# A graph network kernel on one core: the two gathers of a pair wait for the rows of different earlier pairs

## The chip, the cores and the metric

The kernel runs on one core of one Trainium2 chip, in one launch. The metric is the device time of that core in microseconds (us), from three runs of the kernel: median 1267.71 us, from 1265.4 to 1268.62 us. One more execution was recorded by the hardware profiler, and every row below comes from it.

## What is computed

The input is 1250 nodes of 512 features and 20000 edges, sorted by their target node (`dst`). The target nodes are drawn so that low numbers have far more edges. Two graph layers follow each other; the change touches only the scores of the first, an attention over edges (GATv2):

```python
xl = (x @ Wl).reshape(-1, HEADS, C)            # HEADS = 8, C = 64
xr = (x @ Wr).reshape(-1, HEADS, C)
h = jax.nn.leaky_relu(xl[src] + xr[dst], NEG_SLOPE)
e = jnp.einsum('ehc,hc->eh', h, att)           # the score of each edge and head
m = jax.ops.segment_max(e, dst, num_segments=N_NODES)
ex = jnp.exp(e - m[dst])
denom = jax.ops.segment_sum(ex, dst, num_segments=N_NODES)
msg = (ex / (denom[dst] + 1e-16))[..., None] * xl[src]
out = jax.ops.segment_sum(msg, dst, num_segments=N_NODES)
```

After it come a layer norm, a two-layer perceptron with a gelu, and three graph convolutions, all untouched.

## The kernel before, in words

The work is written out by hand, engine by engine: `gpsimd`, `tensor`, `scalar`, `vector` and `sync` each hold the program of one engine, which it runs in the order in which it is written. Engines meet only through counting semaphores. A `Count` is a semaphore with the number that it will have reached; `wait_ge(x.sem, k)` holds an engine until `x` has been raised k times.

The edges are laid in 22528 slots: blocks of 128 target nodes, each padded to whole *pairs*. A pair is 2 x 128 slots, and there are NG = 88 pairs. The left rows (`xl`, 512 numbers and 8 more for the linear part of the score, 520 in all) lie in a table in HBM, `left_table`. The slots that hold no edge read one and the same row of it.

The score stage does, for each pair n:

- GpSimd (`gather`, L567 to L580): two indirect DMAs, one for each 128 slots, which fetch 128 rows of 520 floats each (266240 bytes) into one of DEPTH = 6 buffers `gathered`. Before the first of them it waits until the buffer is free (`sources_kept`, L577), and, from pair 3 on, until `rows_added` has reached n - LEAD + 1 with LEAD = 3, that is until TensorE has added the rows of pair n - 3 (L579). The second gather of a pair has no wait of its own.
- ScalarE (`seed`, L1003 to L1011): waits for both gathers and copies the 128 x 1024 gathered numbers into two of the six PSUM banks of a ring of three pairs (L1010), and the 16 linear numbers aside (L1011, `sources_kept`). After each even pair it also makes the one-hot matrices for the two pairs to come (`target_hots`, L995 and L1000), for which TensorE must have spread the local target numbers (`spread_local`, L695).
- TensorE (`add_right`, L698 to L716): adds the right rows `xr[dst]` to the two banks, as four matmuls of 128x512 (L705: a high and a low part for each bank), and raises `rows_added`; then two small matmuls for the linear part (L714). Ahead of every second pair it does `spread_local` (four matmuls, L695).
- VectorE (L1493 to L1500): waits for `rows_added` of its pair, then multiplies the positive part by the attention vector (L1497) and sums over the channels (L1499).

The wait on `rows_added` at L579 protects no data: the buffers are guarded by `sources_kept`. It limits how far GpSimd runs ahead.

After the stage a softmax over the edges of each target follows, then the message stage, which fetches all the rows again with the same function `gather` (L581 to L586), there without a wait on `rows_added`. Its first six pairs are fetched at the end of the score stage.

Of the kernel before, what the change touches and what calls it, by code (L numbers as in the profile page):

```python
# [52 lines left out]
def build(nc, ins, out):  # L53
# [23 lines left out]
    GROUPS = [range(0, 3), range(3, 7), range(7, NB)]  # L77
    DEPTH = 6

    LEAD = 3  # L80
    DEN = 2 * HEADS + 2
    SPLITS = 2
    TW = D + HEADS
# [15 lines left out]
    with ExitStack() as ctx:  # L99
# [313 lines left out]
        seeded, rows_added, rows_weighted, pair_scored = count("seeded"), count("rows_added"), count("rows_weighted"), count("pair_scored")  # L413
# [120 lines left out]
        def gpsimd(g):  # L534
            g.memset(eps[:, :], LN_EPS).then_inc(*eps_ready.up())
            g.wait_ge(*eps_ready.now())
            g.memset(x_in[PAD_FROM:P, NB - 1, :], 0.0).then_inc(*padded.up())
            g.wait_ge(*padded.now())
            g.memset(back, 0.0).then_inc(*zeros_ready.up())
            g.iota(digits[:, DIGITS_BY_VECTOR:LOW, :], [[1, LOW - DIGITS_BY_VECTOR], [0, EJ]], base=DIGITS_BY_VECTOR, channel_multiplier=0,  # L540
                   allow_small_or_imprecise_dtypes=True).then_inc(*digits_low.up())
            g.memset(ident[:, :], 0.0).then_inc(*go.up())
            g.memset(ones[:, :], 1.0).then_inc(*go.up())
            g.wait_ge(*go.now())
            g.affine_select(out=ident[:, :], in_=ident[:, :], compare_op=ALU.not_equal, fill=1.0,
                            base=0, pattern=[[-1, P]], channel_multiplier=1)
            g.affine_select(out=earlier, in_=ones[:, :], compare_op=ALU.is_ge, fill=0.0,
                            base=-1, pattern=[[1, P]], channel_multiplier=-1)
            g.iota(iota[:, :], [[1, max(NC, EJ)]], base=0, channel_multiplier=0, allow_small_or_imprecise_dtypes=True)
            g.memset(zero[:, :], 0.0)  # L550
            g.iota(minus_own[:, :], [[0, 1]], base=0, channel_multiplier=-1, allow_small_or_imprecise_dtypes=True)
            g.iota(iota_four, [[1, max(NC, EJ)], [0, QUARTET]], base=0, channel_multiplier=0, allow_small_or_imprecise_dtypes=True)
            g.iota(iota_node, [[1, NP]], base=0, channel_multiplier=0, allow_small_or_imprecise_dtypes=True).then_inc(*constants.up())
            g.iota(digits[:, LOW:HIGH, :], [[1, HIGH - LOW], [0, EJ]], base=LOW, channel_multiplier=0,
                   allow_small_or_imprecise_dtypes=True).then_inc(*digits_high.up())

            def scatter(nth):

                g.wait_ge(d_zeros, 32)
                g.wait_ge(moves_ready.sem, 2 * nth + 2)  # L560
                for j in range(SHARE):
                    g.indirect_dma_start(out=moved[nth], out_offset=bass.IndirectOffsetOnAxis(ap=place_i[R0, j:j + 1], axis=0), in_=moving[R0, j, :],  # L562
                                         in_offset=None).then_inc(d_moved[nth], 16)
            scatter(0)
            scatter(1)

            def gather(n):  # L567
                for i in range(2):
                    c = 2 * n + i
                    g.indirect_dma_start(out=gathered[n % DEPTH][:, i, :], out_offset=None, in_=left_table,  # L570
                                         in_offset=bass.IndirectOffsetOnAxis(ap=src_of[:, c:c + 1], axis=0)).then_inc(d_gather[n % DEPTH], 16)
            g.wait_ge(slots_ready.sem, 1)
            for i in range(2):
                g.wait_ge(d_tile[i], 16 * (NB // 2))
            for n in range(NG):
                if n >= DEPTH:
                    g.wait_ge(sources_kept.sem, n - DEPTH + 1)  # L577
                if n >= LEAD:
                    g.wait_ge(rows_added.sem, n - LEAD + 1)  # L579
                gather(n)  # L580
            for n in range(NG):  # L581
                if n < DEPTH:
                    g.wait_ge(sources_kept.sem, max(k for k in range(NG) if k % DEPTH == n) + 1)
                else:
                    g.wait_ge(message.sem, n - DEPTH + 1)
                gather(n)  # L586


            g.wait_ge(flag_ready.sem, 1)
            g.wait_ge(counts_apart.sem, NB - 1)  # L590
            rounded = [counts_rounded.up() for _ in range(NB)]

            def round_counts():
                for b in range(NB):
                    g.wait_ge(hidden_done.sem, ROUND_FROM + b)
                    g.tensor_copy(counts_r[:, b, :], counts[:, b, :]).then_inc(*rounded[b])  # L596

            def keep_counts():
                for b in range(NB):
                    g.wait_ge(most_turned.sem, 1)  # L600
                    if b:
                        g.wait_ge(counts_rounded.sem, b)
                    g.memset(most[:, :], 0.0).then_inc(*rounded[b])
            g.cond(g.value_load(exact_flag[0:1, 0:1], min_val=0, max_val=1), round_counts, keep_counts)
# [1258 lines left out]
        with nc.Block() as block:  # L1863
            block.vector(vector)
            block.scalar(scalar)
            block.tensor(tensor)
            block.gpsimd(gpsimd)
            block.sync(sync)
# [24 lines left out]
```

## Time and profile before

| what | value |
|---|---|
| median of three runs | 1267.71 us (1265.4 to 1268.62) |
| the profiled execution | 1267.25 us |
| its span, first to last instruction | 1265.2 us, so 2.05 us lie outside it |
| score stage, first to last L1497 | 231.8 to 498.1 us of the span |
| busy in the span: TensorE, VectorE, ScalarE, GpSimd | 87%, 81%, 54%, 36% |
| L570, all 352 gathers of both stages | 375.7 us busy, mean 1067 ns; idle before them 206.2 us |
| L1497, 88 of 128x1024 | 107.8 us busy, mean 1225 ns |
| L1499, 88 | 107.4 us busy, mean 1220 ns |
| L1010, 88 of 128x1024 | 90.4 us busy, mean 1028 ns |

A GpSimd row of a gather lasts while GpSimd issues it; the data land later. A row of the timeline gives the start and the length of an instruction, and in brackets how long its engine sat idle before it and what ended that idle time. "issue" there means that the profile shows no releaser. Where an instruction waits for several semaphores, the profile names the one that it takes to be last, and this can be the wrong one: behind L570 it names L1011, whose semaphore had long been raised.

### The profile page before, as it was taken

The page shows a single profiled execution, that of the slowest core. Times are in us where ns is not written, and L with a number is a line of the kernel's source. Part 1 is how long each engine was busy: PE and PEld are TensorE (multiplying, and loading weights), DVE is VectorE, ACT ScalarE, POOL GpSimd, SP SyncE. Part 2 cuts the span into 40 slices and gives each one's busy share as a digit, 9 for nine tenths or more (in the row PEclk, how much of TensorE's full clock was granted, in tenths as well). Part 3 has the DMA queues.
Part 4 walks back from the last instruction along what each step waited for, and adds up shares of the span by engine and source line. Part 5 has one row for each costly group of instructions (what it writes and reads, how often), then busy time and mean ns, then how long its engine had stood idle before and what let it go on. Part 6 is the DMA issues. An engine that isn't in the chain of part 4 may idle for free.

```text
span 1265.2 us, 15650 instructions
## 1 busy us (share of the span) xinstructions
PE 1103.2 (87%) x4847; PEld 815.4 (64%) x4847; DVE 1028.0 (81%) x1458; ACT 678.8 (54%) x1257; POOL 455.9 (36%) x412
## 2 busy tenths in 40 slices
PE   4979878667777775399999999699999999999998
PEld 2578456555556564255555555488888889889896
DVE  8999999778777887899999999876767769573934
ACT  4601200566565663388888888766564674232320
POOL 2072062666665666267777775000002100000000
PEclk9989989676665665599999999799999999999999
DMA  5000000666666667166676776400000111000002
GB/s 189 34 10 15 26 10 7 168 174 175 176 179 169 174 175 183 37 189 194 194 195 195 196 195 142 142 1 26 1 9 26 65 54 31 1 28 15 1 1 83
DMA packets 43434, 122.82 MB, mean 97 GB/s; under 512 B 7838, under 2 KB 8626, under 8 KB 43352
## 3 DMA queue, kind: packets, MB, share of 16 engines
q0 software_dynamic: 29184, 93.81, 28.0%
q1 hardware_dynamic: 14168, 27.98, 6.6%
q8 instruction: 44, 0.72, 0.2%
q14 instruction: 38, 0.31, 0.1%
HBM read 116.13 MB, written 5.59 MB: 96 GB/s over the span
## 4 chain that ended last, share of the span: by engine, by line
PE 46%; ACT 19%; DVE 14%; DMA 7%; issue 7%; POOL 4%; ACTq 1%; SPq 1%; DVEq 0%; POOLq 0%
PE bank L851 11%; PE bank L811 8%; PE bank L797 8%; ACT counts L1037 7%; PE bank L867 7%; DMA arena<-left_table,arena 7%; PE bank L654 5%; POOL arena L570 4%; ACT hot L924 4%; ACT arena L922 4%; PE bank L705 3%; ACT bank L1010 2%; DVE counts L1252 2%; PE bank L759 2%; PE bank L770 1%
## 5 line engine op out<-in xcount | busy, mean ns | idle before, releaser
L570 POOL DMA_INDIRECT arena<-left_table,arena x352 | 375.7, 1067 | 206.2 <-issue 101.6
L759 PE MATMUL bank<-arena,hot 128*128 128x512 f32 x352 | 177.6, 620 | 4.0 <-DVE den_parts L1587 4.0
L705 PE MATMUL bank<-xr_hi,hot_t 128*128 x176 | 114.1, 649 | 73.1 <-ACT bank L1010 50.1
L1497 DVE SCALAR_TENSOR_TENSOR arena<-bank,arena 128x1024 f32<-128x1024 f32 x88 | 107.8, 1225 | 52.3 <-PE bank L705 32.6
L1010 ACT ACTIVATE bank<-arena 128x1024 f32<-128x1024 f32 x88 | 90.4, 1028 | 95.3 <-DMA arena<-left_table,arena 87.3
L851 PE MATMUL bank<-counts_r,ns 128*128 128x512 f32 (+2 forms) x720 | 137.1, 349 | 0.0
L851 PEld LDWEIGHTS bank<-counts_r,ns 128*128 128x128 f32 x720 | 125.6, 188 | 10.4
L1037 ACT ACTIVATE counts<-bank 128x1280 f32 x88 | 108.9, 1238 | 35.0 <-issue 25.8
L770 PE MATMUL bank<-arena 128*128 128x512 bf16 x528 | 113.1, 351 | 0.5 <-ACT counts L1037 0.3
L1499 DVE TENSOR_REDUCE arena<-arena 128x16 f32<-128x1024 f32 x88 | 107.4, 1220 | 3.0
L705 PEld LDWEIGHTS bank<-xr_hi,hot_t 128*128 128x128 f32 x176 | 50.2, 285 | 92.2 <-issue 84.5
L1583 DVE TENSOR_TENSOR arena<-arena 128x1024 f32<-128x1024 f32 x88 | 107.3, 1219 | 0.0
L562 POOL DMA_INDIRECT moved<-counts x32 | 57.7, 1802 | 129.8 <-DVE counts L1301 61.5
L654 PE MATMUL bank<-arena 125*125 125x160 f16 (+1 forms) x576 | 89.8, 332 | 13.9 <-DVE arena L1320 13.9
L760 PE MATMUL bank<-den_parts,hot 128*128 128x18 f32 x176 | 101.9, 579 | 0.0
L705 PE MATMUL bank<-xr_lo,hot_t 128*128 x176 | 100.5, 571 | 0.0
L654 PEld LDWEIGHTS bank<-arena 125*125 125x125 f16 (+1 forms) x576 | 74.9, 157 | 29.2 <-DVE arena L1320 17.4
L1595 DVE TENSOR_SCALAR arena<-arena 128x1280 bf16<-128x1280 f16 x176 | 89.5, 551 | 0.0
L770 PEld LDWEIGHTS bank<-arena 128*128 128x128 bf16 x528 | 52.6, 117 | 53.5 <-ACT counts L1037 14.0
L596 POOL CAST counts_r<-counts 128x1280 fp32r<-128x1280 f32 x10 | 13.6, 1356 | 202.3 <-issue 170.9
L759 PEld LDWEIGHTS bank<-arena,hot 128*128 128x128 f32 x352 | 53.8, 193 | 34.8 <-issue 26.0
L633 PE MATMUL bank<-arena 128*128 128x512 f32 x160 | 75.4, 624 | 0.8 <-ACT arena L917 0.8
(248 smaller groups left out, 2193.8 us busy)
## 6 DMA issues: line engine op xcount, KB each, us to landing
arena<-left_table,arena POOLq DMA_INDIRECT x352
arena<-in_x_dram SPq DMA_DIRECT2D x18, 256.0 KB, 4.6
arena<-in_L_gnn_W_dram SPq DMA_DIRECT2D x8, 512.0 KB
arena<-in_L_gnn_W_dram SPq DMA_DIRECT2D x2, 1536.0 KB, 10.7
arena<-in_L_gnn_W_dram SPq DMA_DIRECT2D x3, 1024.0 KB, 5.2
left_table<-arena SPq DMA_DIRECT2D x10, 260.0 KB, 2.0
out_dram<-state SPq DMA_DIRECT2D x9, 256.0 KB
arena<-in_L_gnn_Wl_dram SPq DMA_DIRECT2D x1, 1024.0 KB, 9.8
```

Of the source, the lines that this page charges most:

```text
L570: g.indirect_dma_start(out=gathered[n % DEPTH][:, i, :], out_offset=None, in_=left_table, in_offset=bass.IndirectOffsetOnAxis(ap=src_of[:, ...
L654: ins_ = t.matmul(bank[0:out_rows, psum, 0:width], rows[R0, at[0], 0:out_rows, at[1]], pick_col[n % 2][R0, at[0], 0:width, at[1]], start=( ...
L705: ins_ = t.matmul(bank[:, 2 * (n % ZRING) + i, :], mine, part[:, bass.ds(at, 1), :].rearrange("p b n -> p (b n)"), start=False, stop=(part ...
L759: t.matmul(bank[:, psum, :], as_float(hot[c % 4]), w[:, i, :], start=(i == 0), stop=(i == 1))
L760: t.matmul(bank[:, psum + 1, 0:DEN], hot[c % 4], den_parts[:, c, :], start=(i == 0), stop=(i == 1)).then_inc(*tile_summed.up())
L770: ins_ = t.matmul(flat[:, COUNT_AT + at:COUNT_AT + end], low_hot[n // 2 % 2][:, :, c % QUARTET], code_hot[c % 4][:, at:end], start=(c == 0 ...
L851: ins_ = t.matmul(bank[:, SUM_BANKS[part][k], 0:n], lhs, rhs, start=(s == 0 and half == 0), stop=(s == NB - 1 and half == 1))
L1010: a.activation(bank[:, at:at + 2, :], gathered[n % DEPTH][:, :, 0:D], ACT.Copy).then_inc(*seeded.up())
L1037: a.activation(counts[:, :, bass.ds(at * P, P)], flat[:, COUNT_AT:COUNT_AT + NP].rearrange("p (b n) -> p b n", n=P), ACT.Copy).then_inc(*c ...
L1497: v.scalar_tensor_tensor(y, bank[:, at:at + 2, :], 0.0, over(att_relu, 1, 2), ALU.max, ALU.mult).then_inc(*rows_weighted.up())
L1499: v.tensor_reduce(sc, y.rearrange("p i (h c) -> p (i h) c", c=C), AX.X, ALU.add).then_inc(*pair_scored.up())
L1583: v.tensor_tensor(w.rearrange("p i (h c) -> p i h c", c=C), gathered[s][:, :, 0:D].rearrange("p i (h c) -> p i h c", c=C), over(weights[:, ...
```

## The change

The one number LEAD = 3 becomes a pair of numbers, 4 for the first gather of a pair and 3 for the second. The wait moves from ahead of the pair into the loop over its two gathers. In the message stage `gather` is called without them and stays as it was.

```diff
-    LEAD = 3
+    LEADS = 4, 3
...
-            def gather(n):
+            def gather(n, rows=None):
+
                 for i in range(2):
                     c = 2 * n + i
+                    if rows and n + 1 - rows[i] > 0:
+                        g.wait_ge(rows_added.sem, n + 1 - rows[i])
                     g.indirect_dma_start(out=gathered[n % DEPTH][:, i, :], out_offset=None, in_=left_table,
                                          in_offset=bass.IndirectOffsetOnAxis(ap=src_of[:, c:c + 1], axis=0)).then_inc(d_gather[n % DEPTH], 16)
...
             for n in range(NG):
                 if n >= DEPTH:
                     g.wait_ge(sources_kept.sem, n - DEPTH + 1)
-                if n >= LEAD:
-                    g.wait_ge(rows_added.sem, n - LEAD + 1)
-                gather(n)
+                gather(n, LEADS)
```

On GpSimd's queue of before, from the seventh gather on (pair 3), the waits stand at the first gather of each pair; `sources_kept` joins from pair 6 on:

```order
L570 DMA arena<-left_table,arena 128x520 [waits tile1_out,tile0_out,slots_ready]
L570 DMA arena<-left_table,arena 128x520 x5
L570 DMA arena<-left_table,arena 128x520 [waits rows_added]
L570 DMA arena<-left_table,arena 128x520
L570 DMA arena<-left_table,arena 128x520 [waits rows_added]
L570 DMA arena<-left_table,arena 128x520
L570 DMA arena<-left_table,arena 128x520 [waits rows_added]
L570 DMA arena<-left_table,arena 128x520
L570 DMA arena<-left_table,arena 128x520 [waits rows_added,sources_kept]
L570 DMA arena<-left_table,arena 128x520
```

The same place after the change (its lines are numbered three higher):

```order
L573 DMA arena<-left_table,arena 128x520 [waits tile1_out,tile0_out,slots_ready]
L573 DMA arena<-left_table,arena 128x520 x6
L573 DMA arena<-left_table,arena 128x520 [waits rows_added] x5
L573 DMA arena<-left_table,arena 128x520 [waits rows_added,sources_kept]
L573 DMA arena<-left_table,arena 128x520 [waits rows_added]
```

One gather more (the first of pair 3) goes without a wait; after it every gather of the stage has a wait on `rows_added`, and the second one of a pair has that alone. No instruction changes its place, on GpSimd or on another engine.

## Rows read from the trace of the kernel before

The windows give, for each stretch, its length and then for TensorE, its weight loads, VectorE, ScalarE and GpSimd the busy time and the number of instructions, then the granted TensorE clock (1.00 is 2.4 GHz, 0.50 is 1.2 GHz), the share of the DMA engines and the GB/s. The waits give the engine and line that waited, for whom, the sum in us, how often, and the longest.

**Rows 1.** Page, part 4: the chain that ended last, by line.
```profile
PE bank L851 11%; PE bank L811 8%; PE bank L797 8%; ACT counts L1037 7%; PE bank L867 7%; DMA arena<-left_table,arena 7%; PE bank L654 5%; POOL arena L570 4%; ACT hot L924 4%; ACT arena L922 4%; PE bank L705 3%; ACT bank L1010 2%; DVE counts L1252 2%; PE bank L759 2%; PE bank L770 1%
```

**Rows 2.** Waits between 230 and 500 us.
```profile
ACT bank L1010 <- DMA arena<-left_table,arena: 87.3, 61, 3.3
...
PE bank L705 <- ACT bank L1010: 50.1, 52, 2.5
DVE arena L1497 <- PE bank L705: 32.6, 43, 1.8
```

**Rows 3.** Timeline of VectorE, L1497 of pair 3 and of pair 87.
```profile
239.41 1.23 DVE L1497 SCALAR_TENSOR_TENSOR arena<-bank,arena 128x1024 f32<-128x1024 f32 x1
...
498.06 1.23 DVE L1497 SCALAR_TENSOR_TENSOR arena<-bank,arena 128x1024 f32<-128x1024 f32 x1 [1.54 <-PE bank L705]
```

**Rows 4.** Timeline, one round of the loop: L1497 of pair 27 to that of pair 30.
```profile
312.26 1.23 DVE L1497 SCALAR_TENSOR_TENSOR arena<-bank,arena 128x1024 f32<-128x1024 f32 x1 [1.04 <-PE bank L705]
...
312.91 0.95 POOL L570 DMA_INDIRECT arena<-left_table,arena  x1 [1.32 <-ACT counts L1011]
...
314.17 0.94 POOL L570 DMA_INDIRECT arena<-left_table,arena  x1 [0.30 <-issue]
...
317.91 1.03 ACT L1010 ACTIVATE bank<-arena 128x1024 f32<-128x1024 f32 x1 [2.30 <-DMA arena<-left_table,arena]
...
319.18 0.79 PE L705 MATMUL bank<-xr_hi,hot_t 128*128 x1 [0.70 <-issue]
...
321.36 1.23 DVE L1497 SCALAR_TENSOR_TENSOR arena<-bank,arena 128x1024 f32<-128x1024 f32 x1 [0.98 <-PE bank L705]
```

**Rows 5.** Windows: the whole stage from pair 3 on, and four stretches.
```profile
239.40:498.10 258.70, 189.37 (x669) 149.69 (x666) 205.41 (x169) 155.40 (x255) 161.19 (x171) 0.61 0.66 176
302.00:308.90 6.90, 3.75 (x21) 2.94 (x20) 6.10 (x6) 4.43 (x8) 4.90 (x6) 0.99 0.70 184
308.90:325.90 17.00, 13.08 (x44) 10.56 (x45) 13.05 (x11) 10.43 (x18) 9.79 (x11) 0.50 0.65 175
...
490.50:503.00 12.50, 4.82 (x15) 3.78 (x13) 9.59 (x9) 2.71 (x5) 9.75 (x10) 0.50 0.83 219
...
473.00:494.00 21.00, 15.90 (x49) 12.43 (x47) 15.61 (x13) 10.31 (x18) 13.33 (x15) 0.50 0.77 161
```

**Rows 6.** Timeline, the step from L1010 to L1497 at the full clock (pair 26).
```profile
306.17 1.03 ACT L1010 ACTIVATE bank<-arena 128x1024 f32<-128x1024 f32 x1 [1.82 <-DMA arena<-left_table,arena]
...
308.74 1.23 DVE L1497 SCALAR_TENSOR_TENSOR arena<-bank,arena 128x1024 f32<-128x1024 f32 x1 [0.48 <-DVE arena L1499]
```

**Rows 7.** Timeline: L1497 of pair 0, and the gather that waits for its rows.
```profile
231.79 1.22 DVE L1497 SCALAR_TENSOR_TENSOR arena<-bank,arena 128x1024 f32<-128x1024 f32 x1 [1.71 <-PE bank L705]
...
232.02 0.95 POOL L570 DMA_INDIRECT arena<-left_table,arena  x1 [3.83 <-PE bank L705]
```

**Rows 8.** Timeline: two L1497 with VectorE never idle between them.
```profile
258.45 1.23 DVE L1497 SCALAR_TENSOR_TENSOR arena<-bank,arena 128x1024 f32<-128x1024 f32 x1 [0.61 <-PE bank L705]
...
260.96 1.23 DVE L1497 SCALAR_TENSOR_TENSOR arena<-bank,arena 128x1024 f32<-128x1024 f32 x1
```

**Rows 9.** Timeline: from the rows of pair 27 over the one-hots to pair 29.
```profile
312.24 0.61 PE L695 MATMUL bank<-arena 128*128 128x128 bf16 x4
...
312.89 0.69 ACT L995 ACTIVATE arena<-bank,minus_own 128x512 f32<-128x512 f32 x1 [0.34 <-PE bank L695]
...
313.69 0.72 ACT L1000 ACTIVATE hot_t<-arena,ones 128x512 fp32r<-128x512 f32 x1
...
314.44 1.03 ACT L1010 ACTIVATE bank<-arena 128x1024 f32<-128x1024 f32 x1
...
317.90 1.23 DVE L1497 SCALAR_TENSOR_TENSOR arena<-bank,arena 128x1024 f32<-128x1024 f32 x1 [0.59 <-PE bank L705]
```

**Rows 10.** Timeline of GpSimd: first and last of nine gathers issued without a wait.
```profile
490.51 0.94 POOL L570 DMA_INDIRECT arena<-left_table,arena  x1 [0.31 <-issue]
...
500.53 0.95 POOL L570 DMA_INDIRECT arena<-left_table,arena  x1 [0.30 <-issue]
```

## The prediction

> **What bounds the kernel now.** I began with the chain that ended last [rows 1]. Of its parts 7% (the data of the gathers on their way), 4% (L570, issuing gathers), 3% (L705) and 2% (L1010) have to do with the stage that the change touches. No compute engine fills this part of the chain: the stage goes at the pace of a round trip. The waits of the stage say the same and show the direction [rows 2]: ScalarE's copy L1010 waits 87.3 us in 61 waits for gathered data, TensorE's L705 waits 50.1 us for that copy, VectorE's L1497 waits 32.6 us for L705. What is late first is the gather.
>
> How long is a pair? L1497 runs once for each pair. From pair 3 to pair 87 are 84 pairs, from 239.41 to 498.06 us [rows 3]: 258.65 us, so 3.08 us for each. From here on "pace" is this number.
>
> Why 3.08? One round trip can be read off the timeline [rows 4]. L1497 of pair 27 begins at 312.26, just as the rows of its pair are done. GpSimd was waiting for these rows and starts the first gather of pair 30 at 312.91 (+0.65), the second at 314.17 (+1.26), ScalarE copies at 317.91 (+3.74, the second gather from its issue to its use; ScalarE sat idle 2.30 us for it), L705 begins at 319.18 and L1497 of pair 30 at 321.36 (+3.45 from the copy). Together 9.10 us for three pairs, since the wait goes three pairs back: 3.03 for one. The measured 3.08 is this loop and 0.05 us for each pair of irregularity. The loop bounds the stage, and the first gather's issue is part of it, although only the second one's data come last.
>
> **The change part by part.** No instruction is added on any engine but the waits, and the gathers, their size and their order stay. What changes is when GpSimd may begin each gather. Name T(n) the start of L1497 of pair n.
>
> 1. The second gather of pair n may begin at T(n-3) plus a wake-up; the first one has gone before it, since it needs only T(n-4). So the 1.26 us of the first issue leave the loop. The first gather itself: T(n-4) + 0.65 + 1.26 is earlier than T(n-3) + 0.2 at any pace above 1.7, so it does not hold up the second.
>
> 2. The wake-up. With two semaphores to wait for it takes 0.65 [rows 4]. The second gather will wait for one alone. The nearest row is the gather of pair 3, which waits for `rows_added` alone: L1497 of pair 0 begins at 231.79, the gather at 232.02 [rows 7], so 0.23. The bounds are 0.23 and 0.65; I take 0.23. The new loop is 0.23 + 3.74 + 3.45 = 7.42 for three pairs, 2.47 for one (2.61 with the dear wake-up). The saving by the loop alone would be 9.10 - 7.42 = 1.68 in three pairs, 0.56 in one. Less than that will arrive, because three other limits lie just below 3.08, and the largest of them takes over:
>
> 3. VectorE. When it is never idle, two L1497 are 258.45 to 260.96 apart [rows 8]: 2.51. GpSimd. Nine gathers issued without a wait, 490.51 to 500.53 [rows 10], are 10.02 / 8 = 1.25 apart, 2.50 for a pair. The extra wait adds nothing when it is already fulfilled, as far as the rows show (the 1.26 in rows 4 is an issue after a two-semaphore wait). In the queue, behind a second gather that waits stands the first one of the next pair: it begins at T(n-3) + 0.23 + 1.25, and the second one after it at T(n-3) + 2.73, against its own release at T(n-2) + 0.23. At a pace of 2.51 both fall together, so GpSimd just keeps up and cannot make up for a delay.
>
> 4. ScalarE and TensorE together. After each even pair ScalarE makes one-hots from a product of TensorE that stands behind the rows of the pair before. With TensorE at the low clock [rows 9]: the rows of pair 27 are there (T = 312.26), L695 runs at 312.24, L995 waits for it and starts at 312.89, L1000 at 313.69, only then the copy of pair 29 at 314.44, and T(29) is 317.90. That is 5.64 us for two pairs, a pace of 2.82, and no earlier gather shortens it. With the full clock the last step is 2.57 (306.17 to 308.74 [rows 6]) in place of 3.45, which alone takes the 5.64 to 4.76, a pace of 2.38 and below VectorE's.
>
> So the pace after the change hangs on TensorE's clock: 2.82 at 1.2 GHz, 2.51 at 2.4 GHz. Before, the granted clock is 0.61 over the stage [rows 5], that is the high level for 22% of the time. In a stretch at the high level TensorE was busy 3.75 of 6.90 us (54%) and it then fell; in one at the low level 13.08 of 17.00 us (77%), and it stayed low [rows 5]. How does the density change? At the low level, 77% at 3.08 becomes 84% at 2.82; at the high one, 54% becomes 66% at 2.51. Both go towards the high level. I take the high level for 0.4 of the time: 0.4 x 2.51 + 0.6 x 2.82 = 2.70. The irregularity of 0.05 should shrink, because a late transfer now finds slack: 3 x 2.82 - 7.42 = 1.04 us at the low level, and at the high one, where the loop is 0.88 shorter, 3 x 2.51 - 6.54 = 0.99. I leave 0.01 of it and take 2.71. Saving: 84 x (3.08 - 2.71) = 31 us. The start gives some more: the first gather of pair 3 no longer waits until 232.02, one issue of 1.25 us in the path to T(3). Sum 32.
>
> The Trainium skill, in "TensorE: Matmul & The Clock Gate" (Part 1: The HAM clock gate), says that the throttled state is the default, that a busy stretch releases it and an idle one brings it back. The direction is that of the two windows above; by that rule alone, with a TensorE that is idle a third of the time at a pace of 2.51, either level could hold, and the saving would be 18 us at the low one and 44 us at the high one, as in the first two rivals.
>
> 5. What comes behind the stage. The six pairs fetched ahead for the message stage are issued after it and are not waited for until the softmax is through; they start earlier by what the stage gains. The softmax and the message stage keep their lengths. So what the stage gains, the end gains.
>
> The sum is made against the profiled execution: 1267.25 us (span 1265.2 and 2.05 outside), less 32 is 1235.2. The median of the runs is 0.46 above that execution; so the prediction is 1235.7.
>
> **The rivals.**
>
> A. The clock stays mostly low. For it: 0.50 for 17 us at a stretch at 77% [rows 5]. Against it: the higher density. Pace 2.82 and 0.05, saving 84 x 0.21 = 18 us: 1250.
>
> B. The clock stays mostly high: 2.51 and 0.05, saving 84 x 0.52 = 44 us: 1224. For it: at the high level every limit other than VectorE and GpSimd is well below 2.51. Against it: it fell at 54%, and 66% isn't far from that.
>
> C. The transfers don't keep up. A pair is 2 x 266240 bytes, at 2.51 us 212 GB/s, where the stage has had 176 [rows 5]. Against it: while gathers were issued at 1.25, 219 GB/s were moved, with the DMA engines 83% busy [rows 5]. If some 190 GB/s is all that holds over a long stretch, the pace is 2.80 and 0.05: saving 19 us, 1248.
>
> D. No change. The copy waits for both gathers, and if the second one's landing depended on something other than its issue, an earlier issue would only lie longer in the queue. The +3.74 would become 3.74 + 1.68, and the time 1268. Against it: DMA engines at 66% busy [rows 5] are idle between the gathers.
>
> E. Slower. More gathers are under way at once, and they hinder each other. In the last pairs of the stage, whose slots read one and the same row, the DMA engines were 77% busy and moved only 161 GB/s [rows 5]. If more transfers in flight pulled the whole stage to that, a pair would take 532480 / 161 = 3.31 us, 84 x 0.23 = 19 us more: 1287. It decides from the point where the rate falls under 532480 / 3.08 = 173 GB/s. Against it: the 219 GB/s, with as many in flight as GpSimd can issue.
>
> **How the numbers follow.** The forecast (a mixed clock) has a chance of 0.47, A 0.16, B 0.18, C 0.10, D 0.05, E 0.04. Faster by over 0.3% (3.8 us, about what the runs can tell from none) are the first four: 0.91. Within 0.3%: 0.05. Slower: 0.04. The likeliest case gives 1235.7. The range goes from B with a little more (1222) to A and C (1252).
>
> **What would show it.** In the profile after: L1497 from pair 3 to 87 in 228 us or so, not 258.65; the second gathers starting 0.2 to 0.3 after an L1497, the first ones 1.25 after the second gather before; L1010's wait for gathered data well under 87.3 us, and in its place ScalarE waiting for L695 and VectorE idle less; the granted clock of the stage above 0.61, at 0.7 to 0.75; 195 to 205 GB/s. I am wrong in step 1 if the time from the second gather to the copy grows by more than a few tenths; in step 2 if the second gathers start 0.65 after L1497 (this alone would cost little); in step 4 if the pace is under 2.8 in stretches at the low clock.

## The result, and the profile after

| | before | after |
|---|---|---|
| median of the runs, us | 1268.16 (4 runs, 1265.4 to 1270.19) | 1234.64 (4 runs, 1232.33 to 1235.81) |
| ratio, 95% interval | | 0.9735 (0.971 to 0.9759) |
| profiled execution, its span | 1267.25, 1265.2 | 1235.52, 1233.6 |
| first gather of the stage to the start of the last sum over the channels | 279.5 us | 247.8 us |
| the softmax behind it | 30.2 us | 30.3 us |
| the message stage, its gathers | 248.1 us | 247.7 us |
| from the last gather to the end | 487.6 us | 487.5 us |

The whole gain of the profiled executions (31.6 us of span) lies in the score stage (31.7 us), as step 5 had it. Ratios leave out slow runs, of which there was one (leads_3_3 below: 1770.64 us at a granted clock of 0.552). In the new kernel the lines are one further down from L571 on: the copy is L1011, the rows L706, VectorE's product L1498; a gather is L573.

VectorE's timeline, product of pair 0, 3 and 87 (start, length, engine, line, and in brackets the idle time before it and what ended it), kernel after:

```profile
231.45 1.22 DVE L1498 SCALAR_TENSOR_TENSOR arena<-bank,arena 128x1024 f32<-128x1024 f32 x1 [0.82 <-PE bank L706]
...
239.95 1.22 DVE L1498 SCALAR_TENSOR_TENSOR arena<-bank,arena 128x1024 f32<-128x1024 f32 x1
...
466.91 1.23 DVE L1498 SCALAR_TENSOR_TENSOR arena<-bank,arena 128x1024 f32<-128x1024 f32 x1 [0.99 <-PE bank L706]
```

From pair 3 to 87 that is 226.96 us and a pace of 2.70, against 258.65 and 3.08 in [rows 3]. Of the 84 distances between two products 64 are 2.51 to 2.55, those of a VectorE that is hardly ever idle; before there were 17.

The waits of the kernel after between 230 and 470 us (sum, times, longest), which answer to [rows 2]:

```profile
PE bank L706 <- ACT bank L1011: 68.4, 58, 3.1
...
ACT bank L1011 <- DMA arena<-left_table,arena: 45.2, 46, 2.5
...
ACT arena L996 <- PE bank L696: 19.3, 22, 1.9
DVE arena L1498 <- PE bank L706: 18.2, 21, 1.6
```

The copy's wait for data is down from 87.3 to 45.2 us, VectorE's from 32.6 to 18.2, and ScalarE waits 19.3 us for the product that it makes the one-hots from.

One delay and what follows it, timeline of the kernel after:

```profile
247.65 0.95 POOL L573 DMA_INDIRECT arena<-left_table,arena  x1 [0.30 <-issue]
...
252.53 1.22 DVE L1498 SCALAR_TENSOR_TENSOR arena<-bank,arena 128x1024 f32<-128x1024 f32 x1
...
253.20 1.03 ACT L1011 ACTIVATE bank<-arena 128x1024 f32<-128x1024 f32 x1 [1.63 <-DMA arena<-left_table,arena]
...
256.65 1.22 DVE L1498 SCALAR_TENSOR_TENSOR arena<-bank,arena 128x1024 f32<-128x1024 f32 x1 [1.64 <-PE bank L706]
256.81 0.94 POOL L573 DMA_INDIRECT arena<-left_table,arena  x1 [1.80 <-PE bank L706]
...
257.27 0.69 ACT L996 ACTIVATE arena<-bank,minus_own 128x512 f32<-128x512 f32 x1 [1.61 <-PE bank L696]
```

The second gather of pair 9 is issued at 247.65 and its copy begins 5.55 us later, where [rows 4] have 3.74: a transfer that is late, and VectorE stands still for 1.64 us. GpSimd, which in most rounds issues without a stop, waits for the rows of pair 9 and goes on 0.16 us after the product has begun. This is the second gather of pair 12, released three pairs back, with the cheap wake-up of [rows 7].

Windows of the kernel after: the stage from pair 3 to about 82, the rest with its last five pairs, then two stretches at the low clock and one at the high one (columns as in [rows 5]):

```profile
239.90:447.50 207.60, 149.41 (x627) 120.99 (x626) 191.79 (x158) 147.29 (x240) 148.34 (x157) 0.75 0.73 201
447.50:466.90 19.40, 12.43 (x40) 9.83 (x38) 13.53 (x12) 8.00 (x14) 12.85 (x14) 0.59 0.99 195
...
280.30:290.60 10.30, 9.15 (x30) 7.39 (x31) 8.84 (x8) 6.00 (x10) 6.87 (x8) 0.50 0.68 188
417.24:425.30 8.06, 6.98 (x23) 5.76 (x24) 7.33 (x6) 5.05 (x10) 5.67 (x6) 0.50 0.76 217
328.10:334.90 6.80, 3.92 (x22) 3.14 (x22) 6.63 (x6) 5.43 (x9) 5.28 (x6) 1.00 0.73 201
```

In the long window VectorE is busy for 92% (191.79 of 207.60), and the clock is at 0.75, where the stage had 0.61. The last five pairs are another matter: DMA engines busy 99%, VectorE 70%.

### The profile page after: what moved, and what is told of

It reads as the page before. It is cut to its first block, busy times and chain, and to the rows that moved or that the text cites. A ratio compares the mean times of both kernels' runs of the same rounds, so it can differ in the third digit from the quotient of the medians.

```text
span 1233.6 us, 15630 instructions
## 1 busy us (share of the span) xinstructions
PE 1073.8 (87%) x4827; PEld 796.7 (65%) x4847; DVE 1027.9 (83%) x1458; ACT 679.6 (55%) x1257; POOL 455.7 (37%) x412
## 4 chain that ended last, share of the span: by engine, by line
PE 49%; ACT 22%; DVE 15%; DMA 6%; issue 4%; POOL 2%; ACTq 2%; SPq 1%; DVEq 0%; POOLq 0%
PE bank L852 11%; PE bank L812 9%; PE bank L798 8%; ACT counts L1038 8%; PE bank L868 7%; PE bank L655 5%; DMA arena<-left_table,arena 5%; PE bank L706 4%; ACT hot L925 4%; ACT arena L923 4%; ACT bank L1011 3%; POOL arena L573 2%; DVE counts L1253 2%; PE bank L760 2%; ACT hot_t L1001 1%
## 5 line engine op out<-in xcount | busy, mean ns | idle before, releaser
L573 POOL DMA_INDIRECT arena<-left_table,arena x352 | 376.2, 1069 | 173.6 <-issue 93.9
L706 PE MATMUL bank<-xr_hi,hot_t 128*128 x176 | 102.7, 584 | 68.8 <-ACT bank L1011 68.4
L1498 DVE SCALAR_TENSOR_TENSOR arena<-bank,arena 128x1024 f32<-128x1024 f32 x88 | 107.7, 1224 | 20.7 <-PE bank L706 18.2
L1011 ACT ACTIVATE bank<-arena 128x1024 f32<-128x1024 f32 x88 | 90.4, 1028 | 49.3 <-DMA arena<-left_table,arena 45.2
L771 PE MATMUL bank<-arena 128*128 128x512 bf16 (+1 forms) x508 | 109.6, 348 | 2.4 <-DVE arena L1596 0.4
L706 PEld LDWEIGHTS bank<-xr_hi,hot_t 128*128 128x128 f32 x176 | 45.4, 258 | 83.1 <-issue 76.3
L706 PE MATMUL bank<-xr_lo,hot_t 128*128 x176 | 89.5, 509 | 0.0
```

Of the source, the lines that this page charges most:

```text
L706: ins_ = t.matmul(bank[:, 2 * (n % ZRING) + i, :], mine, part[:, bass.ds(at, 1), :].rearrange("p b n -> p (b n)"), start=False, stop=(part ...
L771: ins_ = t.matmul(flat[:, COUNT_AT + at:COUNT_AT + end], low_hot[n // 2 % 2][:, :, c % QUARTET], code_hot[c % 4][:, at:end], start=(c == 0 ...
L1011: a.activation(bank[:, at:at + 2, :], gathered[n % DEPTH][:, :, 0:D], ACT.Copy).then_inc(*seeded.up())
L1498: v.scalar_tensor_tensor(y, bank[:, at:at + 2, :], 0.0, over(att_relu, 1, 2), ALU.max, ALU.mult).then_inc(*rows_weighted.up())
```

## The experiments

Each was compared with the kernel before on the same chip. The first four ran on one chip, the next four on a second, three on a third, the last on a fourth. "Before" had medians of 1262.88, 1262.56, 1264.37 and 1265.33 us on them.

**leads_3_3: the new code with the old distances.**

```diff
-    LEADS = 4, 3
+    LEADS = 3, 3
```

> Both gathers of a pair wait for the pair three back, the second with a wait of its own that the first has already fulfilled. Loop theory: the first gather's release (0.65 us) and its issue (1.25 us) are back in the loop, 9.1 us for three pairs, so the pace is 3.08 us again and the time that of the kernel before, 1268 us, within 3. Rival (the gain comes from the form of the waits, not from the pair that they name): close to 1235 us.

Measured: 1263.5 us, ratio 1.0004 (0.9991 to 1.0018), pace 3.06. The new form of the waits costs nothing by itself; with the second gather's wait already fulfilled by the first one's, the old loop is back. (The changed kernel itself did not run on this chip, so the first four experiments are compared with it by their ratios to before.)

**leads_3_2: both gathers one pair tighter than the change.**

```diff
-    LEADS = 4, 3
+    LEADS = 3, 2
```

> First gather three back, second two back. Loop theory: the second gather is held to 0.2 us after the rows of two pairs back, 0.2 + 3.74 + 3.45 = 7.4 us for two pairs, a pace of 3.7 us at TensorE's low clock and 3.3 at the high one; with the clock low 84 x 0.65 = 55 us over the kernel before, about 1322 us. Rival (VectorE or GpSimd is the bound, and the gathers' release matters little): 1268 us or less.

Measured: 1308.86 us, ratio 1.0364 (1.034 to 1.0388), pace 3.59: 46 us over the kernel before, where 55 were expected. Its timeline, a round of two pairs:

```profile
310.91 1.22 DVE L1498 SCALAR_TENSOR_TENSOR arena<-bank,arena 128x1024 f32<-128x1024 f32 x1 [1.33 <-PE bank L706]
311.08 0.95 POOL L573 DMA_INDIRECT arena<-left_table,arena  x1 [1.62 <-PE bank L706]
...
314.90 1.03 ACT L1011 ACTIVATE bank<-arena 128x1024 f32<-128x1024 f32 x1 [1.62 <-DMA arena<-left_table,arena]
...
318.38 1.22 DVE L1498 SCALAR_TENSOR_TENSOR arena<-bank,arena 128x1024 f32<-128x1024 f32 x1 [1.75 <-PE bank L706]
```

From the product at 310.91 the gather goes 0.17 later, its copy 3.82 after that, the next but one product 3.48 after the copy: 7.47 us. This is the loop of steps 1 and 2 (forecast 7.42), here laid over two pairs: 3.73 for one by this round, 3.59 by the mean. The loop and its wake-up are shown by it, since here it bounds the stage.

**leads_4_4: the second gather looser too.**

```diff
-    LEADS = 4, 3
+    LEADS = 4, 4
```

> Both gathers four back. Loop theory: 9.1 us for four pairs, 2.28, below VectorE's 2.51 as the loop with 4 and 3 already is, so nothing more is to be had but slack for late transfers: 1230 to 1236 us. Rival (the loop of the second gather is still the bound with 4 and 3): the remaining gap of 2.70 to 2.51, 16 us, goes: 1219 us. Rival (more gathers in flight hinder each other): over 1240 us.

Measured: 1225.43 us, ratio 0.9699 (0.9683 to 0.9716), pace 2.58. Of the 84 distances 76 are 2.51; the pairs 3 to 82 go at 2.54, the last five at 3.24. By its ratio this would be 1230 us in the session of the result, the edge of the first expectation: slack for late transfers is worth more than it said. Over 1240 us, as crowding gathers would have it, it is not.

**leads_6_6: as loose as the buffers allow.**

```diff
-    LEADS = 4, 3
+    LEADS = 6, 6
```

> The wait on rows is for the pair six back, so only the six buffers hold GpSimd (released when the linear numbers of the pair six back are copied). If slack for late transfers is worth something beyond four back: 1228 to 1234 us. If gathers in flight hinder each other, it shows here most: over 1240 us, with a longer time from a gather's issue to its copy that holds up L1011 (L1010 before). At the end of the stage, where all slots read one row, GpSimd runs furthest ahead and the transfers queue.

Measured: 1220.2 us, ratio 0.9667 (0.9648 to 0.9687), pace 2.535, and 2.68 in the last five pairs. Its waits between 230 and 454 us:

```profile
PE bank L706 <- ACT bank L1011: 58.4, 49, 1.8
...
ACT arena L996 <- PE bank L696: 36.4, 34, 1.9
ACT bank L1011 <- DMA arena<-left_table,arena: 7.4, 5, 2.5
```

Hardly anything is left of the wait for data (7.4 us, 45.2 in the changed kernel), and the pairs 3 to 82 go at 2.53 in place of 2.65. The sum of that wait is not by itself the price: leads_4_4 still has 36.3 us of it and goes at 2.54. What costs is the single transfer so late that VectorE stops for it. Here TensorE's rows are done up to 3.8 us before VectorE takes them, and 80 of the 84 distances are 2.51: VectorE's own time is what is left. The transfers move 212 GB/s over the whole stage here:

```profile
231.00:453.00 222.00, 164.09 (x694) 135.07 (x692) 213.28 (x175) 159.60 (x264) 166.56 (x177) 0.73 0.78 212
```

It has the lowest ratio of all versions, 0.9667 against the change's 0.9735 (which was measured in another session).

**after_again: the changed kernel, unchanged, on the second chip.**

> The changed kernel itself again, beside the three that follow on the same chip. A ratio of 0.9735 to before, within 0.003.

Measured: 1260.32 us (12 runs, 1251.59 to 1267.94), ratio 0.9981 (0.9957 to 1.0004), pace 3.04. The gain is not there, and all runs are far above the 1235.81 that was the slowest in the session of the result. VectorE's products in its timeline:

```profile
259.64 1.23 DVE L1498 SCALAR_TENSOR_TENSOR arena<-bank,arena 128x1024 f32<-128x1024 f32 x1 [1.81 <-remote]
...
262.15 1.22 DVE L1498 SCALAR_TENSOR_TENSOR arena<-bank,arena 128x1024 f32<-128x1024 f32 x1
...
264.68 1.23 DVE L1498 SCALAR_TENSOR_TENSOR arena<-bank,arena 128x1024 f32<-128x1024 f32 x1
...
267.19 1.23 DVE L1498 SCALAR_TENSOR_TENSOR arena<-bank,arena 128x1024 f32<-128x1024 f32 x1
...
271.21 1.23 DVE L1498 SCALAR_TENSOR_TENSOR arena<-bank,arena 128x1024 f32<-128x1024 f32 x1 [1.55 <-PE bank L706]
```

Three distances of 2.51 and one of 4.02, and so on: up to 329 us every fourth pair has such a stop. What VectorE waits for is not late by the records. The same view with TensorE, around 343 us:

```profile
339.48 0.61 PE L696 MATMUL bank<-arena 128*128 128x128 bf16 x4
...
341.27 0.63 PE L706 MATMUL bank<-xr_lo,hot_t 128*128 x1
...
343.77 0.69 ACT L996 ACTIVATE arena<-bank,minus_own 128x512 f32<-128x512 f32 x1 [4.14 <-remote]
343.90 1.23 DVE L1498 SCALAR_TENSOR_TENSOR arena<-bank,arena 128x1024 f32<-128x1024 f32 x1 [1.16 <-remote]
344.06 0.95 POOL L573 DMA_INDIRECT arena<-left_table,arena  x1 [1.44 <-remote]
```

TensorE's product for the one-hots ends at 340.09, the last of the rows at 341.90. ScalarE, VectorE and GpSimd, each with nothing else to do, go on at 343.77, 343.90 and 344.06: 3.7 us after the end of the first, and 2.0 and 2.2 us after that of the rows. "Remote" is a releaser that the profile does not show. I call this a late signal, after what the records show; the ends of matmuls are modelled in them, so matmuls that really ended later would look the same. I count as one a product before which VectorE sat idle although its rows had ended over 0.25 us earlier. There are 23 in the 85 pairs from 3 to 87 here. The profiles of before, after, leads_3_3, leads_3_2, leads_4_4 and leads_6_6 have none. VectorE sat idle for 32.3 us before those 23 products, and from pair 3 to 87 this kernel took 28.1 us longer than in the session of the result (255.10 to 226.96). The granted clock from pair 3 to 82 is lower too, 0.65 to 0.75; whether as a cause or a consequence is open.

**pads_apart: the changed kernel, but slots without an edge read different rows.** A slot without an edge fetches the row with its partition's number, not one and the same row. VectorE has two small instructions more, ahead of the stage.

```diff
+            own_row = high_i.bitcast(F32)
+            v.tensor_scalar(own_row, key[:, :], 0.0, minus_own[:, :], ALU.is_equal, ALU.mult).then_inc(*vo.up())
+            v.wait_ge(*vo.now())
+            v.tensor_tensor(src_of[:, :], src_of[:, :], own_row, ALU.subtract).then_inc(*vo.up())
+            v.wait_ge(*vo.now())
```

> The changed kernel, in which the slots without an edge gather the row of their own partition number in place of all one row (two VectorE instructions more ahead of the stage, 0.5 us). Theory: the last five pairs of the score stage are 3.6 us apart, against 2.65 before them, because transfers that all read one row are slow; with rows apart they come at 2.6, 5 us less, and the time from the issue of their gathers to the copy falls from 5.9 to 3.8. Rival: the end of the stage is slow for another reason (the gathers of the next stage queue beside them), and nothing changes.

Measured: 1267.96 us (1255.49 to 1274.23), ratio 1.0028 (1.0005 to 1.0051): no gain, rather a loss. Its profiled execution is one of its short ones (span 1253.3) and can't stand for the median; why that median is 7.6 us above that of after_again was not found. The windows of the last 20 us of the stage (the last seven pairs here, five and a bit in after_again), first this kernel's:

```profile
467.20:487.30 20.10, 13.81 (x50) 11.27 (x50) 17.58 (x16) 10.97 (x19) 13.54 (x15) 0.67 0.68 189
```

and of after_again:

```profile
476.50:496.00 19.50, 13.89 (x43) 10.88 (x40) 14.75 (x13) 8.68 (x16) 13.27 (x14) 0.51 0.99 196
```

The DMA engines are no longer full (0.68, not 0.99). By the DMA packets the gathers of the last five pairs are through 3.1 to 3.5 us after their issue, against 4.0 to 6.5 in after_again, and the five pairs go at 2.83 in place of 3.42. So the full DMA engines at the end of the stage do come from the one row that all empty slots read; either kernel has one late signal in these five pairs. What it is worth on a chip without late signals stays open; 5 x (3.61 - 2.51) = 5.5 us is the most it could be in the changed kernel, less than the spread of this kernel's runs.

**spread_early: TensorE makes the product for the one-hots one pair earlier.**

```diff
-                if n % 2 == 0 and n < NG - 2:
-                    spread_local(n // 2 + 1)
+                if n == 0:
+                    spread_local(1)
+                elif n % 2 == 1 and n < NG - 3:
+                    spread_local((n + 3) // 2)
```

> The changed kernel, with TensorE's spread of the local target numbers (L696) one pair earlier in its order, so that ScalarE never waits for it (19.3 us in the changed kernel). The prediction's step 4 had this loop bound the pace at 2.82 at the low clock. If it does, the pairs at the low clock go from 2.74 to 2.51 and the stage gets some 9 us shorter. Rival (it costs only right behind a late transfer, three times 0.6 us): 2 us less or no difference.

Measured: 1254.82 us, ratio 0.9936 (0.9919 to 0.9954), pace 2.97 against 3.04 for the changed kernel on that chip, with 22 late signals. It is the one kernel that gained over 0.3% on this chip. That a late signal holds back the one-hots less when their product was made earlier would explain it; this was not tried by itself. On this chip the run can't decide what it was made for, the loop of step 4; leads_6_6 does (below).

**half_reduce: the changed kernel, VectorE sums half of the channels only.**

```diff
-                v.tensor_reduce(sc, y.rearrange("p i (h c) -> p (i h) c", c=C), AX.X, ALU.add).then_inc(*pair_scored.up())
+                v.tensor_reduce(sc, y.rearrange("p i (h c) -> p (i h) c", c=C)[:, :, 0:C // 2], AX.X, ALU.add).then_inc(*pair_scored.up())
```

> The changed kernel, leaving out half of the channels in VectorE's sum (L1500), so that its two instructions take 1.9 us a pair in place of 2.5. If VectorE alone bounds the changed stage: 40 us less. If GpSimd's two issues of 1.25 us bound it just as much, as the prediction says: the pace stays at 2.50 and above, 0 to 6 us less, from delays that VectorE now makes up for.

Measured: 1260.79 us, ratio 0.9972 (0.9952 to 0.9992), pace 3.045, 27 late signals. VectorE has 0.53 us less to do for each pair (a sum takes 0.69 us in place of 1.22), and the time is the same within 0.3%: it does not bound the stage on that chip. Where there are no late signals this was not run.

**before_copy, after_third, leads_6_6_again: three kernels as they were, on a third chip.** I now had two theories for the missing gain. By the first, that chip is slower for every kernel in this stage. By the second, late signals come only where the stage runs denser than before.

> The kernel before, unchanged, for its profile on the chip on which the next two run. In the last four runs VectorE found the rows of a pair signalled some 1.6 us after TensorE's recorded end in 22 or 23 of 85 pairs, and the changed kernel was no faster than before (0.998). Theory 1 (a trait of that chip that hits every kernel): on such a chip this one has such pairs too. Theory 2 (they come only where the stage runs at the denser pace): this one has none on any chip. Ratio 1.000.

> The changed kernel a third time. On a chip without the late signals 0.9735 to before, a pace of 2.70, no late signal; on one with them 0.998, a pace of 3.0 and a late signal in about every fourth pair.

> Both gathers six back, again, beside the changed kernel. On a chip without the late signals 0.967, and 0.993 to the changed kernel; on one with them it can do nothing against a late signal of TensorE, since the rows then wait for nothing that a gather brings: 0.99 to 1.00 of before.

| | us | ratio (95%) | pace | late signals of 85 |
|---|---|---|---|---|
| before_copy | 1262.74 | 0.9988 (0.9974 to 1.0002) | 3.05 | 1 |
| after_third | 1265.41 | 1.0006 (0.9981 to 1.0031) | 3.08 | 24 |
| leads_6_6_again | 1262.52 | 0.9993 (0.9977 to 1.0009) | 3.05 | 18 |

The waits of leads_6_6_again between 230 and 500 us:

```profile
PEld bank L706 <- issue: 96.3, 45, 7.0
PE bank L706 <- ACT bank L1011: 56.7, 24, 6.6
...
ACT arena L996 <- remote: 44.1, 11, 7.7
PE bank L706 <- issue: 35.4, 20, 7.0
DVE arena L1498 <- remote: 26.7, 12, 6.7
```

It waits for no data, but 44.1 and 26.7 us for releasers that the profile does not show. The first theory fell: the kernel before runs at its usual pace here, with one late signal. The second, which expected none, holds but for that one. With looser waits, of either distance, the late signals come and take the whole gain.

**static_block: fewer instructions on TensorE for each pair.** The number of the block is read once, so every pair adds the right rows of block 0.

```diff
-                at = t.value_load(block_of[0:1, n:n + 1], min_val=0, max_val=NB - 1)
+                at = first_block
...
             t.wait_ge(right_split.sem, NB)
+            first_block = t.value_load(block_of[0:1, 0:1], min_val=0, max_val=NB - 1)
```

> The changed kernel, but TensorE reads the number of the block once, before the stage, and not for each pair: a load of a register, its two index instructions and what belongs to them are left out for each pair (435 instructions in all), so every pair adds the right rows of block 0. The matmuls, their count and their shapes stay. Theory S (TensorE's signals are late because of how many instructions its sequencer gets through, each with a record): on a chip where the changed kernel shows VectorE idle about 1.6 us in every fourth pair behind rows that are long done, fewer instructions for a pair give fewer such gaps (under 15 of 85 in place of 23 or 24) and a pace under 2.85 us in place of 3.04 to 3.08, so the time is 15 us or more under the kernel before. Theory W (they are late for another reason, whatever TensorE's instructions are): 20 to 25 such gaps and a pace of 3.0 to 3.1, within 4 us of the kernel before. On a chip without such gaps both expect the changed kernel's time, 0.97 to 0.975 of the kernel before, a pace of 2.70 or a little less (a register load fewer ahead of the rows), and the question stays open.

Measured: 1227.98 us (5 runs, 1225.92 to 1228.08), ratio 0.9698 (0.9678 to 0.9718), pace 2.63, no late signal. The fourth chip is of the kind without them, or the fewer instructions took them away; the two can't be told apart, since the changed kernel itself did not run there. So it confirms neither S nor W. Its gain is like that of the change, a little larger: the pairs 3 to 82 go at 2.58, not 2.645.

## Why the prediction was right

It gave 1235.7 us, and the runs 1234.64; the profiled execution has 1235.52 for the forecast 1235.2. Point by point:

- **Step 1 held.** The second gather is released three pairs back, and the first issue of 1.26 us has left the loop. leads_3_3 brings it back and with it the whole 3.06; leads_3_2 makes the new loop bind and shows it at 7.47 us for 7.42 forecast. That a second gather can land no earlier (rival D) is excluded in the same way: its copy came 3.82 after its issue in that round, against 3.74.
- **Step 2 held.** A second gather that waits starts 0.16 to 0.23 us after the product: 256.65 to 256.81 above. I had said that most would wait. In most rounds GpSimd issues one every 1.25 us instead, and the second gather's wait is just fulfilled when it gets to it. This is the tie of step 3, and it cuts the other way too: a GpSimd at its limit can't make up for a delay.
- **Step 3 held.** 64 of 84 distances are at most 2.55. That it is VectorE which bounds them is shown by leads_6_6, where its rows lie ready up to 3.8 us ahead; that GpSimd's 2.50 would be the next bound was not tested.
- **Step 4 had the right rate and made the wrong use of it, and this did not show in the sum.** I took 2.82 as the pace at the low clock. Of the 79 distances up to pair 82, 14 lie wholly at the low clock and average 2.81, 31 wholly at the high one and average 2.51; the other 34 hold a change of level and average 2.70. But no long stretch goes at 2.82. The 5.64 us of [rows 9] come again right behind a stop of VectorE: the products of pairs 10 and 11 are 2.51 and 3.12 behind the one before, 5.63 together. Elsewhere the same clock gives 2.51, 2.51 and then 3.04, as for pairs 71 to 73; these are the products of pairs 69 to 73, and the fourth window above, at a clock of 0.50, is the stretch from 70 to 73:

```profile
414.73 1.22 DVE L1498 SCALAR_TENSOR_TENSOR arena<-bank,arena 128x1024 f32<-128x1024 f32 x1
...
417.24 1.22 DVE L1498 SCALAR_TENSOR_TENSOR arena<-bank,arena 128x1024 f32<-128x1024 f32 x1
...
419.75 1.22 DVE L1498 SCALAR_TENSOR_TENSOR arena<-bank,arena 128x1024 f32<-128x1024 f32 x1
...
422.26 1.22 DVE L1498 SCALAR_TENSOR_TENSOR arena<-bank,arena 128x1024 f32<-128x1024 f32 x1
...
425.30 1.22 DVE L1498 SCALAR_TENSOR_TENSOR arena<-bank,arena 128x1024 f32<-128x1024 f32 x1 [0.56 <-PE bank L706]
```

  What I missed is the buffer between the engines. At the high clock TensorE finishes its rows up to 1.5 us before VectorE takes them, and the low stretch behind it uses up this lead: 1.14 us before the product at 417.24, 0.18 before the next. The sign that I had named, a pace under 2.8 at the low clock, is not in the 2.81 of this kernel but in leads_6_6: 26 distances wholly at the low clock average 2.55 there, 23 of them 2.51. So the loop of step 4 does not bound the stage while TensorE is ahead. In the sum it is a small thing: the granted clock from pair 3 to 82 was 0.75, that is the high level for 0.5 of the time, not 0.4, and with 0.5 the prediction's own mix gives 2.665, against 2.645 measured.
- **The slack for late transfers was too large with it.** I had 1.04 us at the low clock, from a pace of 2.82; at 2.51 it is 3 x 2.51 - 7.42 = 0.11. Nearly all that the changed kernel loses against 2.51 up to pair 82 lies in 14 distances over 2.7 (10.3 us together), and seven of these pairs (9, 20, 25, 43, 54, 63, 73) have a second gather that landed 4.4 to 5.5 us after its issue, where the median is 3.8. leads_4_4, which gives the second gather a pair more, has four such distances, 2.2 us in all.
- **Rival E was right about the place.** In the last five pairs the pace was 3.61: all slots without an edge read one row. Before, these pairs went at 3.41 and hid behind a stage that wasn't much faster. The forecast had no term for them.
- **The errors cancel.** 79 pairs at 2.645 in place of 2.71 are 5.1 us less; five pairs at 3.61 are 4.5 us more. The 228 us that I gave for pair 3 to 87 became 226.96. The prediction's number is better than its reasons.
- **The start gave nothing.** From the first gather to the product of pair 3 are 19.6 us before and after (219.8 to 239.41, 220.3 to 239.95); the 1 us forecast did not come, and could not: before, the products of pair 0 and pair 3 are already 7.62 us apart (231.79 to 239.41), and three of VectorE's 2.51 are 7.53.
- **Rival C did not come.** The stage moved 201 GB/s, and 212 in leads_6_6. Single late transfers are what is left of it.
- **What the list of rivals lacked** is the result of the second and third chip. There the time was that of rival D, by a mechanism that nothing in the trace of before pointed to. The 0.9735 holds for the session in which it was measured; leads_4_4, leads_6_6 and static_block show gains of 3.0 to 3.3% for the same loop on two further chips, and on two others the gain was zero.

The Trainium skill, "TensorE: Matmul & The Clock Gate" (Part 1: The HAM clock gate), has a busy TensorE released and an idle one throttled. The windows above agree in direction: TensorE was 89% busy (9.15 of 10.30) at the low level, and the high one followed; it was 58% busy (3.92 of 6.80) at the high level, and the low one followed. The level went back and forth through the stage. Neither level held, so neither of the two times that this rule alone gave in the prediction came true.

## What to carry to other kernels

In a loop that is limited by a round trip, count which issues lie between its release and its last arrival, and give each issue its own release: the first half can go earlier at no cost. When several limits lie within 10% of each other, look for how much an engine can run ahead before adding up the slowest step of each state; a step's rate bounds the stage only once that lead is used up. And measure a gain of this kind on more than one chip: here the same kernel gave 2.7% in one session and nothing in two others.

## What the runs showed of the hardware

- **Late signals.** On two chips about every fourth pair of a dense stage has the engines that wait for TensorE going on together, long after TensorE's recorded end: VectorE 0.4 to 2.9 us after the rows in after_again, up to 8 us in leads_6_6_again and 9 us in after_third and half_reduce. From 259.6 to 329.4 in after_again they come every 11.6 us. Their cost is about the whole gain: VectorE is idle 32.3 us before the 23 of after_again, and the change had brought 31. They appear in every denser kernel on these chips, in none of those on the chips of the result and of the first four experiments, and not with the distances of before (one in before_copy). Moving TensorE's product (22) or easing VectorE (27) does not change their number by much.
- **What goes with them.** The six traces without any late signal of versions other than before hold 10941 to 10943 records of semaphore changes; the six with many hold 6909 to 7263, the two of the kernel before 7903 and 7791. Whether the loss of records and the delay have one cause was not settled, and two things speak against it. The first trace of the kernel before has only 7903 and no late signal. And the message stage loses them as well without getting longer: between 550 and 700 us, inside it, after_again has 1240 records and after 2289, and its gathers take 247.9 and 247.7 us. Whether the recording of a run has itself a part in the delays was not tested.
- **Gathers of one row.** In the last five pairs of the changed kernel, where gathers read one row in all their empty slots, a gather takes 4.9 to 8.2 us from issue to landing, with the DMA engines 99% busy; the median before them is 3.8. With different rows in the empty slots (pads_apart) the DMA engines are 68% busy there. leads_6_6 hides most of it (2.68 in place of 3.61), since its gathers start earlier.
